# First stage in another order: the mask's copy, the choice of chunks, and the low part of the query weights

## The chip, the cores and the metric

One core of one Trainium2 chip. The core has TensorE (PE: matrix products and transposes), VectorE (DVE), ScalarE (ACT), GpSimd (POOL) and SyncE (SP), which issues the DMAs here. Each engine runs its own instructions in order and waits on semaphores for the others. The metric is the time of one execution on the device in microseconds (us).

## The reference

A Perceiver-like layer in float32. Only the first step matters here.

```
x: (16, 64, 512)   ctx: (16, 1601, 512)   mask: (1, 1, 64, 1601), int32, 0 = hidden
n = (x - mean) / sqrt(var + 1e-5)
q = n @ w_q.T ; k = ctx @ w_k.T ; v = ctx @ w_v.T          16 heads of 32
s = q . k / sqrt(32) ; s = where(mask == 0, -1e9, s)
x = x + softmax(s) @ v @ w_o.T
x = x + self-attention of norm(x) with LoRA terms
x = x + gated mixture of 20 experts (top 2) of norm(x)
```

With the given inputs the mask is 0 for the first part of the keys and 1 behind it, the same for all 64 queries.

## The kernel before

The keys are padded to 2000 and cut into 5 chunks of 400. The program looks at the mask and works out which chunks hold an unmasked key for some query; only those are computed. In the given data one chunk is left, and the branches for more chunks are jumped over.

Products in full float32 accuracy are made of three matmuls in the faster type float32r: each operand is split in a high part (a rounding copy, on ScalarE) and a low part (source minus high part, on VectorE, `rest`). `mm3` issues the three (lines 186 to 188). `weight_hi` and `weight_lo` do this for whole weights of 128x2048, `turn_x` for the transposed x, `context` for the context.

The first stage runs as follows.

- SyncE (`sync`) issues, in this order, the constants, the mask in two copies (one for partitions 0 to 63, one for 64 to 127, into the room of `qc`, named `mska`), the first half of x, wq, the second half of x, wk, and the LoRA factors. The mask's copy reads `in_mask`, laid out chunk by chunk, so that a partition's row of 2000 words comes in 5 pieces of 1600 bytes. Then SyncE waits for `v_ids` 4, loads the chunk's number from `ids` and issues the context of the first batch element (`craw`), two copies for `cap` and one for `excl`, then, behind `v_w` 1, wv into the room of wq.
- VectorE waits for the mask, reduces it to one flag per chunk (`cm`, L1092), makes a flag for rows without any key (`rows`), and writes `fl`. TensorE transposes `fl` into bank 7 (L263), VectorE reduces it to `fr`, TensorE multiplies it with a triangle of ones (L265), VectorE reads the result into `frow` (L1108), and twelve small instructions (L1111 to L1119) turn it into the list of chunks and their count, `ids`. The statistics of x tiles 0 and 1 (`bn`, L1079 and L1081) lie in the gaps of this exchange.
- Then VectorE does the statistics of tiles 2 and 3, the variance (L1085), waits for GpSimd's power -0.5 (L1631), scales (L1124), normalises tiles 0 and 1 (`apply_x`, L1088), makes wq's low part, and takes the four transposed tiles as they come (`turn_x`). After these come the context's low part, wk's low part, the same work for x tiles 4 to 7, wv's low part, `make_cap`, and the LoRA factors' blocks (L1294, L1297).
- TensorE transposes the tiles (L192), multiplies the LoRA factors (L420), does the query products of tiles 0 to 3 (`queries(0)`, 48 matmuls), transposes tiles 4 and 5, does two of four key products of the first batch element, transposes tiles 6 and 7, does the other two, and then `queries(1)`. Behind that is the loop over 16 batch elements (`cross(0)`).
- ScalarE makes wq's high part, copies the four transposed tiles, then the context's high part, wk's and wv's, and then empties the banks of the query products.
- GpSimd does nothing in this stage but the two powers (`power`); afterwards it scales the attention's weights.

`v_w` counts low parts of weights made on VectorE; wk's is the second, wv's the third, wo's the fourth. The order on each engine is written by hand.

Near the end the mixture of experts gathers tokens with GpSimd's DMAs into `xi`, a ring of X = 11 buffers, X - 1 of them ahead.

## Time and profile before

| | |
|---|---|
| median of 3 runs | 786.26 us (784.39 to 786.62) |
| profiled execution | 786.06 us |
| its span | 784.2 us |
| PE busy | 710.7 us (91%) |
| DVE busy | 412.2 us (53%) |
| ACT busy | 362.4 us (46%) |
| POOL busy | 280.5 us (36%) |
| DMA | 72.61 MB, mean 93 GB/s |

The times of the trace are counted from the span's start. PE is the engine of the matmuls; PEld are its weight loads, which run beside them; SPq is the queue of SyncE, which issues DMAs. A timeline line gives start, duration, engine, line of the code, operation, what is written and read with its shape, the number of instructions merged into the line, and in brackets how long the engine had stood idle before and what ended that. A line of busy time by stretch gives from:to, the length, the busy time (and number of instructions) of PE, PEld, DVE, ACT and POOL in this order, the granted clock of TensorE as a share of 2.4 GHz, the busy share of the 16 DMA engines, and the GB/s that they moved. The list of DMA issues gives the number of copies, the size of one and the median time from issue to landing.

### The profile page before, as it was taken

Reading aid. Unit: us, or ns where it says so; the run is one execution under the profiler, and the core shown is the slowest. Engines: PE = TensorE matmul, PEld = TensorE weight load, DVE = VectorE, ACT = ScalarE, POOL = GpSimd, SP = SyncE. Lnnn points to the kernel's source line nnn. Section 1 sums busy time; section 2 is a strip of 40 time slices with the busy share of each in tenths; the row PEclk is TensorE's granted clock in tenths of the full one; section 3 lists DMA queues with packets and bytes.
Section 4 is the critical chain, followed back from the end, with each engine's and each line's share of the span. In section 5 each row is a group of like instructions: output and inputs, shape, how many; then the busy total and the mean of one; then the engine's idle time right before and its main releaser. Section 6 shows DMA issues by size and latency. Waiting matters only on the chain.

```text
span 784.2 us, 17023 instructions
## 1 busy us (share of the span) xinstructions
PE 710.7 (91%) x6845; PEld 586.5 (75%) x6845; DVE 412.2 (53%) x950; ACT 362.4 (46%) x662; POOL 280.5 (36%) x256
## 2 busy tenths in 40 slices
PE   0899999999999999999999999999999745999970
PEld 0697888878878887889887877887778644788860
DVE  4833344453444324544454236635476557599965
ACT  1425344553545344534454244434365240499950
POOL 0005145413553245324542353613125212566530
PEclk9999999999999999999999999999999975799995
DMA  9401101211121101110110002110001753499918
GB/s 288 148 1 43 44 2 44 97 69 35 38 97 43 44 1 43 43 44 2 43 43 3 2 3 73 59 63 2 2 17 43 267 186 133 166 373 389 338 53 321
DMA packets 29585, 72.61 MB, mean 93 GB/s; under 512 B 3917, under 2 KB 4941, under 8 KB 28472
## 3 DMA queue, kind: packets, MB, share of 16 engines
q1 hardware_dynamic: 25096, 63.00, 22.9%
q0 software_dynamic: 4400, 8.41, 3.0%
q8 instruction: 58, 0.95, 0.5%
q14 instruction: 31, 0.25, 0.1%
HBM read 66.14 MB, written 11.27 MB: 99 GB/s over the span
## 4 chain that ended last, share of the span: by engine, by line
PE 85%; DVE 5%; issue 4%; ACT 2%; DMA 2%; SPq 0%; POOL 0%; DVEq 0%; POOLq 0%; ACTq 0%
PE bank L186 22%; PE bank L188 20%; PE bank L187 20%; PE bank L192 10%; PE bank L345 4%; PE bank L322 3%; DMA wr<-scratch_ys 1%; PE bank L644 1%; PE bank L560 1%; PE bank L656 1%; PE bank L547 1%; PE bank L576 1%; DVE wh L1072 1%; DVE stats L1326 0%; ACT wh L751 0%
## 5 line engine op out<-in xcount | busy, mean ns | idle before, releaser
L1641 POOL TENSOR_SCALAR pp<-pp,rl 128x400 f32<-128x400 f32 x128 | 163.8, 1297 | 234.8 <-DVE rl L1169 234.8
L1224 DVE COPY pt<-bank 128x512 f32<-128x512 f32 x64 | 44.3, 692 | 99.4 <-PE bank L192 99.3
L186 PE MATMUL bank<-chi,wk 128*128 128x400 f32 x256 | 93.5, 365 | 0.0
L834 ACT ACTIVATE pp<-pp,acc 128x400 f32<-128x400 f32 x128 | 79.0, 620 | 28.0 <-DVE acc L1257 27.7
L1257 DVE CUSTOM_DVE_ANT_0 pp<-bank,cap 128x400 f32<-128x400 f32 x128 | 66.8, 569 | 46.5 <-PE bank L322 46.5
L188 PE MATMUL bank<-chi,wk 128*128 128x400 f32 x256 | 88.3, 345 | 0.0
L187 PE MATMUL bank<-clo,wk 128*128 128x400 f32 x256 | 88.3, 345 | 0.0
L186 PE MATMUL bank<-wv,chi 128*128 128x512 f32 x200 | 83.5, 417 | 0.0
L188 PE MATMUL bank<-wv,clo 128*128 128x512 f32 x200 | 78.5, 393 | 0.0
L187 PE MATMUL bank<-wv,chi 128*128 128x512 f32 x200 | 78.5, 393 | 0.0
L751 ACT ACTIVATE pt<-bank 128x512 f32<-128x512 f32 x64 | 38.2, 597 | 76.4 <-PE bank L192 75.3
L192 PE MATMUL bank<-cst,pp 128*128 128x128 f32 x512 | 67.2, 274 | 0.6 <-DVE x_sb L1201 0.6
L186 PE MATMUL bank<-wh,xu 128*128 128x512 f32 x152 | 65.1, 428 | 1.0 <-issue 1.0
L192 PEld LDWEIGHTS bank<-cst,pp 128*128 128x128 f32 x512 | 58.5, 140 | 5.8 <-issue 0.8
L188 PE MATMUL bank<-wh,xu 128*128 128x512 f32 x152 | 61.8, 407 | 0.0
L187 PE MATMUL bank<-wh,xu 128*128 128x512 f32 x152 | 61.6, 405 | 0.0
L751 ACT ACTIVATE vv<-bank 128x512 f32<-128x512 f32 x50 | 29.1, 583 | 65.0 <-PE bank L188 65.0
L186 PEld LDWEIGHTS bank<-wv,chi 128*128 128x128 f32 x200 | 37.5, 187 | 28.0 <-issue 19.4
L1156 DVE COPY kk<-bank 128x400 f32<-128x400 f32 x32 | 18.4, 575 | 63.3 <-PE bank L188 63.3
L187 PEld LDWEIGHTS bank<-clo,wk 128*128 128x128 f32 x256 | 48.3, 189 | 0.0
L186 PEld LDWEIGHTS bank<-chi,wk 128*128 128x128 f32 x256 | 48.2, 188 | 0.0
L188 PEld LDWEIGHTS bank<-chi,wk 128*128 128x128 f32 x256 | 48.1, 188 | 0.0
(244 smaller groups left out, 1394.2 us busy)
## 6 DMA issues: line engine op xcount, KB each, us to landing
wr<-in_We SPq DMA_DIRECT2D x13, 1024.0 KB
craw<-in_ctx SPq DMA_DIRECT2D x16, 800.0 KB, 4.3
raw<-in_We SPq DMA_DIRECT2D x8, 1024.0 KB
acc<-in_We SPq DMA_DIRECT2D x6, 1024.0 KB
wr<-scratch_ys SPq DMA_DIRECT2D x8, 512.0 KB, 7.6
x_sb<-in_x SPq DMA_DIRECT2D x2, 1024.0 KB, 11.8
scratch_xn<-acc SPq DMA_DIRECT2D x8, 256.0 KB, 2.6
out_dram<-x_sb SPq DMA_DIRECT2D x8, 256.0 KB, 5.7
```

The costliest lines, as they stand in the source:

```text
L186: pe.matmul(o, lhs[0], rhs[0], start=start, stop=False)
L187: pe.matmul(o, lhs[0], rhs[1], start=False, stop=False)
L188: return pe.matmul(o, lhs[1], rhs[0], start=False, stop=stop)
L192: last = pe.transpose(bank[0:n, k * 128:(k + 1) * 128], of(k), ident)
L322: last = pe.matmul(scores[64 * c:64 * c + 64, j, :], qc[r, 2 * half + c, 64 * b:64 * b + 64], kk[r, 2 * half + c, :], start=True, stop=True)
L345: last = pe.matmul(turned[32 * j:32 * j + 32, g, :], vv[:, (25 * (n // 8) + 3 * (n % 8) + i4) % 4, 128 * g + 32 * j:128 * g + 32 * j + 32] ...
L751: return act.activation(dst, src, ACT.Copy)
L834: act.activation(frame(p8), frame(p8), ACT.Exp, bias=bias, scale=-1.0, accum_out=total).then_inc(S["a_exp"], 1)
L1156: dve.tensor_copy(kk[:, g, :], at("k", 4 * n + g)[:, 0:CW]).then_inc(S["v_k"], 1)
L1224: dve.tensor_copy(pt[:, p8 % 4, :, :].rearrange("p a c -> p (a c)"), at("t", 8 * (n - 1) + p8)[:, :]).then_inc(S["v_pt"], 1)
L1257: dve.tensor_tensor_reduce(out=frame(p8), in0=scores[:, p8 % 4, :], in1=cap[:, :], scale=-1.0, scalar=nm[:, b, p8:p8 + 1] if seg else 3e38 ...
L1641: pool.tensor_scalar(frame(p8), frame(p8), rl[:, n % 2, p8:p8 + 1], None, ALU.mult).then_inc(S["g_pn"], 1)
```

## The change

Five edits, all but the last in the first stage.

1. The mask is read from a new input `rows`, the same data laid out by query, so that a partition's row is one piece of 8000 bytes. `cap` still reads `in_mask`.
2. On VectorE all four bn pairs and the variance come directly behind `rows`; `fl` is made behind the variance, `fr` behind that, `frow` is read behind the second normalise.
3. The twelve small instructions that make `ids` are a function `used()`, called behind the fourth `turn_x`, in front of the context's low part.
4. wq's low part is made on GpSimd, behind the first power, in four instructions of 128x512, with its own semaphore `g_w`. The counts of `v_w` fall by one. SyncE's copy of wv waits for `g_w`. TensorE does `queries(0)` before the LoRA products instead of behind them.
5. X, the number of `xi` buffers, is 10 instead of 11.

```diff
--- before.py
+++ after.py
@@ -21,7 +21,7 @@
     NB, D, T, CW, PW, NC_, E, X8 = 16, 512, 1024, 400, 112, 5, 20, 15
     EPS = 1e-5
     SCALE = 32.0 ** -0.5
-    R, X, EARLY, SPLIT, BLOCKS = 8, 11, 4, 9, 35
+    R, X, EARLY, SPLIT, BLOCKS = 8, 10, 4, 9, 35
     LAST, LEAD = E + X8, 96
 
     root = ExitStack()
@@ -164,7 +164,7 @@
 
 
         names = """d_cst d_x0 d_x1 d_ctx d_cap d_xn d_raw0 d_raw1 d_par
-            v_own p_ids v_ids g_rstd v_mv v_var v_xn p_xt a_xt v_xt a_w v_w p_q a_q g_own g_zero
+            v_own p_ids v_ids g_rstd v_mv v_var v_xn p_xt a_xt v_xt a_w g_w v_w p_q a_q g_own g_zero
             a_ctx v_ctx p_k a_k v_k p_v a_v p_s v_max a_exp p_t a_pt v_pt p_pv v_o v_cap v_cor a_cor v_rl g_pn v_dg p_dg  v_lora s_bar
             a_h v_h g_h p_o v_x1 s_redo v_r g_r g_ln a_nx p_n a_n v_n2 p_wl a_wl v_wl p_bl v_bl p_qd a_qd v_qd
             p_kT a_kT p_v2 a_v2 a_w2 v_w2 g_we g_xb p_sc v_sm a_e2 v_rl2 g_p2 p_t2 a_t2 p_a2 a_h2 v_h2 p_pj v_x2 p_n2 a_n2
@@ -271,7 +271,7 @@
                 turn4(pe, pb[5 + i % 2], lambda k: xn[:, i % 2, k * 128:(k + 1) * 128]).then_inc(S["p_xt"], 1)
 
             def queries(hf):
-                pe.wait_ge(S["v_w"], 1)
+                pe.wait_ge(S["g_w"], 1)
                 pe.wait_ge(S["v_xt"], 4 * hf + 4)
                 for m in range(4):
                     for ready in freed("q", 4 * hf + m):
@@ -283,7 +283,7 @@
 
             def k_part(n, g):
                 c = columns(n)
-                pe.wait_ge(S["v_w"], 2)
+                pe.wait_ge(S["v_w"], 1)
                 pe.wait_ge(S["v_ctx"], n + 1)
                 for ready in freed("k", 4 * n + g):
                     pe.wait_ge(*ready)
@@ -293,7 +293,7 @@
                 last.then_inc(S["p_k"], 1)
 
             def v_part(n, j):
-                pe.wait_ge(S["v_w"], 3)
+                pe.wait_ge(S["v_w"], 2)
                 if j % 25 % 3 == 0 and j % 25 not in (0, 24):
                     pe.wait_ge(S["v_ctx"], n + 2)
                 for ready in freed("v", j):
@@ -414,13 +414,13 @@
 
             for i in range(4):
                 turn_x(i)
+            queries(0)
             pe.wait_ge(S["d_par"], 16)
             pe.wait_ge(S["v_ids"], 3)
             for j in range(2):
                 last = pe.matmul(pb[7][:, j * 128:(j + 1) * 128], lora[:, 2 * j, :], lora[:, 2 * j + 1, :], start=True,
                                  stop=True)
             last.then_inc(S["p_ids"], 1)
-            queries(0)
             turn_x(4)
             turn_x(5)
             k_part(0, 0)
@@ -1095,28 +1095,21 @@
             dve.wait_ge(own.sem, own.n)
             own.on(dve.tensor_reduce(rows[:, 0:1], cm[:, :], AX.X, ALU.max))
             dve.wait_ge(own.sem, own.n)
-            dve.tensor_scalar(rows[:, 1:2], rows[:, 0:1], SCALE, None, ALU.mult)
+            own.on(dve.tensor_scalar(rows[:, 1:2], rows[:, 0:1], SCALE, None, ALU.mult))
             own.on(dve.tensor_scalar(rows[:, 2:3], rows[:, 0:1], -1.0, 1.0, ALU.mult, ALU.add))
-            dve.wait_ge(own.sem, own.n)
-            dve.tensor_scalar(fl[:, 0:NC_], cm[:, :], rows[:, 2:3], None, ALU.max).then_inc(S["v_ids"], 1)
-            dve.wait_ge(d_x[0], 16)
-            own.on(bn(0))
-            dve.wait_ge(S["p_ids"], 1)
-            dve.tensor_reduce(fr[:, :], pb[7][0:NC_, 0:128], AX.X, ALU.max).then_inc(S["v_ids"], 1)
-            own.on(bn(1))
-            dve.wait_ge(S["p_ids"], 2)
-            dve.tensor_copy(frow[:, 0:10], pb[7][0:1, 0:10]).then_inc(S["v_ids"], 1)
-            dve.wait_ge(S["v_ids"], 3)
             dve.wait_ge(S["d_cst"], 16)
-            own.on(dve.tensor_tensor(frow[:, 10:15], frow[:, 0:5], cst[0:1, 142:147], ALU.mult))
-            for j in range(NC_):
+
+            def used():
+
+                own.on(dve.tensor_tensor(frow[:, 10:15], frow[:, 0:5], cst[0:1, 142:147], ALU.mult))
+                for j in range(NC_):
+                    dve.wait_ge(own.sem, own.n)
+                    own.on(dve.scalar_tensor_tensor(out=frow[:, 15:20], in0=frow[:, 5:10], scalar=float(j + 1),
+                                                    in1=frow[:, 10:15], op0=ALU.is_equal, op1=ALU.mult,
+                                                    accum_out=frow[:, 20 + j:21 + j]))
                 dve.wait_ge(own.sem, own.n)
-                own.on(dve.scalar_tensor_tensor(out=frow[:, 15:20], in0=frow[:, 5:10], scalar=float(j + 1),
-                                                in1=frow[:, 10:15], op0=ALU.is_equal, op1=ALU.mult,
-                                                accum_out=frow[:, 20 + j:21 + j]))
-            dve.wait_ge(own.sem, own.n)
-            dve.tensor_copy(ids[:, 0:5], frow[:, 20:25]).then_inc(S["v_ids"], 1)
-            dve.tensor_copy(ids[:, 5:6], frow[:, 9:10]).then_inc(S["v_ids"], 1)
+                dve.tensor_copy(ids[:, 0:5], frow[:, 20:25]).then_inc(S["v_ids"], 1)
+                dve.tensor_copy(ids[:, 5:6], frow[:, 9:10]).then_inc(S["v_ids"], 1)
 
 
             def scaled(i, n):
@@ -1267,17 +1260,24 @@
                             share(n, p8 // 2 - 1, seg)
                     share(n, 3, seg)
 
-            own.on(bn(2))
-            own.on(bn(3))
+            dve.wait_ge(d_x[0], 16)
+            for i in range(4):
+                own.on(bn(i))
             variance(0, 4)
+            dve.tensor_scalar(fl[:, 0:NC_], cm[:, :], rows[:, 2:3], None, ALU.max).then_inc(S["v_ids"], 1)
+            dve.wait_ge(S["p_ids"], 1)
+            dve.tensor_reduce(fr[:, :], pb[7][0:NC_, 0:128], AX.X, ALU.max).then_inc(S["v_ids"], 1)
             scaled(0, 4)
             apply_x(0)
             apply_x(1)
-            weight_lo(wh[0], raw[:, 0], 1)
+            dve.wait_ge(S["p_ids"], 2)
+            dve.tensor_copy(frow[:, 0:10], pb[7][0:1, 0:10]).then_inc(S["v_ids"], 1)
             for i in range(4):
                 turn_x(i)
                 if i < 2:
                     apply_x(i + 2)
+            dve.wait_ge(S["v_ids"], 3)
+            used()
             context(0)
             weight_lo(wk, raw[:, 1], 2)
             dve.wait_ge(d_x[1], 16)
@@ -1642,6 +1642,11 @@
                                            ALU.mult).then_inc(S["g_pn"], 1)
 
             power(0, 4, (S["v_var"], 1), S["g_rstd"])
+            pool.wait_ge(S["a_w"], 1)
+            pool.wait_ge(d_raw[0], 16)
+            for k in range(4):
+                ins = pool.tensor_tensor(wh[0][1][:, k, :], raw[:, 0, k, :], wh[0][0][:, k, :].bitcast(f32), ALU.subtract)
+            ins.then_inc(S["g_w"], 1)
             power(4, 4, (S["v_var"], 2), S["g_rstd"])
             pool.wait_ge(S["p_q"], 8)
             alone(pool.memset(pp[:, 0:8 * D].rearrange("p (t c) -> p t c", t=8)[:, :, 0:PW], 0.0))
@@ -1752,7 +1757,7 @@
         def sync(sp):
             sp.dma_start(cst[:, :], t["cst"]).then_inc(S["d_cst"], 16)
             for h in range(2):
-                sp.dma_start(mska[64 * h:64 * h + 64, :, :], t["mask"].rearrange("c q k -> q c k")).then_inc(S["d_cap"], 16)
+                sp.dma_start(mska[64 * h:64 * h + 64, :, :], t["rows"]).then_inc(S["d_cap"], 16)
             xv = t["x"].rearrange("(i b) q d -> i (b q) d", b=2)
             sp.dma_start(x_sb[:, 0:4, :], xv[0:4].rearrange("i p d -> p i d")).then_inc(d_x[0], 16)
             sp.dma_start(raw[:, 0], t["wq"]).then_inc(d_raw[0], 16)
@@ -1789,18 +1794,18 @@
                 for b in range(NB - 1):
                     context(16 * seg + b + 1, b + 1, chunk)
                     if seg == 0 and b == 4:
-                        sp.wait_ge(S["v_w"], 3)
+                        sp.wait_ge(S["v_w"], 2)
                         sp.dma_start(raw[:, 0], t["wo"]).then_inc(d_raw[0], 16)
                     if seg == 0 and b == 5:
                         sp.dma_start(raw[:, 1], t["w2q"]).then_inc(d_raw[1], 16)
                     if seg == 0 and b == 7:
-                        sp.wait_ge(S["v_w"], 4)
+                        sp.wait_ge(S["v_w"], 3)
                         sp.dma_start(raw[:, 0], t["w2k"]).then_inc(d_raw[0], 16)
 
             chunk = chunk_of(0)
             context(0, 0, chunk)
             load_cap(chunk, 0)
-            sp.wait_ge(S["v_w"], 1)
+            sp.wait_ge(S["g_w"], 1)
             sp.dma_start(raw[:, 0], t["wv"]).then_inc(d_raw[0], 16)
             sp.wait_ge(S["v_ids"], 5)
             count = sp.value_load(ids[0:1, 5:6], min_val=1, max_val=5)
@@ -1973,6 +1978,7 @@
         "x": v["x"],
         "ctx": ctx.reshape(16, NC, CW, 4, 128).transpose(0, 1, 4, 3, 2),
         "mask": mask.reshape(64, NC, CW).transpose(1, 0, 2),
+        "rows": mask.reshape(64, NC, CW),
         "excl": excl,
         "cst": cst,
         "cs2": cs2,
```

## Rows read from the trace of the kernel before

**Rows 1.** the page's chain of work that ended last, its share of the span by engine.

```profile
PE 85%; DVE 5%; issue 4%; ACT 2%; DMA 2%; SPq 0%; POOL 0%; DVEq 0%; POOLq 0%; ACTq 0%
```

**Rows 2.** busy time of each engine by stretch (columns as told above).

```profile
28.00:41.00 13.00, 13.00 (x49) 10.27 (x49) 11.38 (x17) 5.59 (x6) 1.02 (x1) 1.00 0.19 64
...
60.00:475.00 415.00, 413.04 (x4453) 341.69 (x4452) 175.35 (x460) 189.54 (x428) 164.82 (x130) 1.00 0.11 37
```

**Rows 3.** the same view, three stretches of the first 23 us.

```profile
2.50:10.00 7.50, 0.00 (x0) 0.00 (x0) 0.00 (x0) 0.00 (x0) 0.00 (x0) 1.00 0.98 220
...
10.00:15.00 5.00, 0.57 (x3) 0.16 (x3) 4.78 (x12) 0.04 (x1) 0.00 (x0) 1.00 1.03 403
...
21.00:23.00 2.00, 1.23 (x6) 0.83 (x4) 2.00 (x2) 1.19 (x2) 0.00 (x0) 1.00 0.87 219
```

**Rows 4.** timeline of VectorE, 10 to 18 us.

```profile
10.02 2.24 DVE L1092 TENSOR_REDUCE cm<-qc 128x5 f32<-128x2000 int32 x1 [10.02 <-DMA qc<-in_mask]
...
12.94 0.23 DVE L1101 TENSOR_SCALAR fl<-cm,rows 128x5 f32<-128x5 f32 x1
...
15.03 0.15 DVE L1111 TENSOR_TENSOR frow<-frow,cst 1x5 f32<-1x5 f32 x1
...
16.33 0.67 DVE L1079 BATCH_NORM_STATS2 stats<-x_sb 128x6 f32<-128x512 f32 x1
...
18.05 0.17 DVE L1085 TENSOR_SCALAR rstd<-mv 128x4 f32<-128x4 f32 x1
```

**Rows 5.** DMA of the context: SyncE's timeline, and the list of issues.

```profile
17.35 0.36 SPq L1770 DMA_DIRECT2D craw<-in_ctx  x1
...
craw<-in_ctx SPq DMA_DIRECT2D x16, 800.0 KB, 4.3
```

**Rows 6.** timeline, all engines, 19 to 28 us.

```profile
19.66 1.00 DVE L1088 TENSOR_SCALAR xn<-x_sb,mv,rstd 128x512 f32<-128x512 f32 x2
...
20.26 1.97 PE L192 MATMUL bank<-cst,xn 128*128 128x128 f32 x8 [5.87 <-DVE xn L1088]
...
21.41 0.60 ACT L751 ACTIVATE xt<-bank 128x512 fp32r<-128x512 f32 x1 [4.54 <-PE bank L192]
...
23.38 0.54 DVE L1088 TENSOR_SCALAR xn<-x_sb,mv,rstd 128x512 f32<-128x512 f32 x1
...
26.80 0.69 DVE L1072 TENSOR_TENSOR xt<-bank,xt 128x512 fp32r<-128x512 f32 x1 [0.36 <-ACT xt L751]
...
27.64 0.77 PE L186 MATMUL bank<-xt,wh 128*128 128x512 f32 x1 [0.36 <-DVE xt L1072]
```

**Rows 7.** timeline, all engines, 26 to 48 us.

```profile
26.67 1.53 ACT L751 ACTIVATE chi<-craw 128x1600 fp32r<-128x1600 f32 x1
...
28.23 1.83 DVE L1072 TENSOR_TENSOR clo<-craw,chi 128x1600 fp32r<-128x1600 f32 x1 [0.73 <-ACT chi L751]
...
32.24 0.69 DVE L1079 BATCH_NORM_STATS2 stats<-x_sb 128x6 f32<-128x512 f32 x1
...
37.14 1.00 DVE L1088 TENSOR_SCALAR xn<-x_sb,mv,rstd 128x512 f32<-128x512 f32 x2
...
40.94 1.03 PE L192 MATMUL bank<-cst,xn 128*128 128x128 f32 x8
...
43.92 0.54 DVE L1088 TENSOR_SCALAR xn<-x_sb,mv,rstd 128x512 f32<-128x512 f32 x1
...
47.01 0.43 PE L186 MATMUL bank<-chi,wk 128*128 128x400 f32 x1
```

**Rows 8.** groups of GpSimd's instructions: count | busy us, mean ns of one | idle before.

```profile
L1704 POOL TENSOR_TENSOR wh<-raw,wh 128x512 fp32r<-128x512 f32 x4 | 5.1, 1290 | 0.0
```

**Rows 9.** TensorE's idle time and clock near 618 us: timeline, then stretches.

```profile
618.06 0.66 PE L192 MATMUL bank<-cst,acc 128*128 128x128 f32 x4 [2.38 <-ACT acc L901]
...
615.80:619.20 3.40, 1.14 (x7) 1.06 (x8) 0.40 (x3) 1.26 (x2) 0.74 (x2) 1.00 1.00 288
...
619.20:622.60 3.40, 3.40 (x9) 2.67 (x9) 2.38 (x6) 0.15 (x1) 0.58 (x2) 0.50 1.05 386
```

## The prediction, made blind

> **What bounds the kernel now.** I read the chain of waits first: TensorE has 85% of it [rows 1]. Then the busy times by stretch: from 28 to 41 us TensorE is busy in all of 13.00 us, and from 60 to 475 us in 413.04 of 415 [rows 2]. So from the first query product at 27.64 [rows 6] to the end of the attention over the chosen chunk TensorE hardly waits, and whatever shifts it in the first stage shifts the end by as much. The change touches nothing behind that but one buffer (11 to 10 of `xi`). The question is when TensorE starts, and how long it idles afterwards. The clock column tells a second thing: after TensorE had been busy for 1.14 of 3.40 us (an idle 2.38 us among them) the granted clock fell to 0.50 for the next 3.4 us, the lower of its two levels, 1.2 GHz [rows 9]. Idle time can cost twice.
>
> **The start of VectorE.** It waits for the mask until 10.02 [rows 4]. Call the mask's landing m. The copy's two halves write 64 partitions each. In 2.5 to 10 us the 16 DMA engines moved 220 GB/s, in 10 to 15 us, x and the query weights on 128 partitions, 403 [rows 3]. Spread over 16 engines, a piece of 1600 B at 220 GB/s takes 116 ns and a piece of 2048 B of x at 403 takes 81 ns: the shorter piece is slower, so its length can't be the whole reason. The stretch of the next copies on 64 partitions (`cap`) shows 219 again [rows 3]. New copy: pieces of 8000 B, still 64 partitions. The mask is 128 x 2000 words of 4 B [rows 4], 1.02 MB. Ends for m: 10.0 (nothing gained; 10.6 if four long pieces per engine balance worse) and 7.0 (the 1.02 MB at 403 instead of 220 GB/s saves 2.1 us, and up to 0.9 more for fewer pieces). The nearest row is `cap`'s, so I stay near the upper end: m = 9.1. x comes right behind: 1.05 MB at 403 GB/s are 2.6 us, less than the 2.92 us that VectorE needs from m to the end of the `rows` work (10.02 to 12.94 [rows 4]).
>
> The Trainium skill, "SBUF — State Buffer", section "Door 1: The DMA port swizzle", says that bandwidth goes by how many of 16 ports the partitions reach, and its formula gives 64 neighbouring partitions half of them. By that rule a longer piece brings hardly anything, m is 9 to 10, and it speaks against this part of the change. The two rates of rows 3 (220 and 403) agree with it; no row separates it from the length of the pieces.
>
> **The order on VectorE.** Behind the 2.92 us come four bn pairs: the last two take 16.33 to 18.05, 0.86 each, so 3.44. From the variance to the first normalised tile there are 18.05 to 19.66, 1.61 [rows 4, 6]; GpSimd's power lies in it, and over it now lies the round of `fl`, TensorE and `fr`, which hides there (one transpose and a short reduce; up to 0.2 us if not). Sum: first tile at m + 8.0 = 17.1, before 19.66. Taken out of this path are the reads of `frow` and `ids` (15.03 to 16.33, six small operations and two casts [rows 4]).
>
> From the first tile to the third were 3.72 us, with the low part of the query weights between; without it VectorE waits for nothing but the hand-overs TensorE, ScalarE, VectorE. Normalising starts 0.6 ahead of its transposes (19.66, 20.26), ScalarE's copy follows 1.15 later (21.41) and takes 0.6, the subtraction 0.7: 3.05 us [rows 6]. From there to the end of the last subtraction 23.38 to 27.49 [rows 6], 4.1. So the four transposed tiles are ready at m + 15.1 = 24.2 and the queries start at 24.3, 3.3 us earlier than now.
>
> **GpSimd.** Four subtractions of 128x512 at 1.290 us, the same operation and types as in [rows 8], are 5.2 us. They begin behind the power at m + 7.6 and end at m + 12.8, 2.3 us ahead of the tiles: costs nothing. At 1.5 us each it still ends ahead. If this cover goes, the queries start later by the rest, and that falls into the idle time shown below, so up to 3 us late it would still cost nothing.
>
> **What is moved behind.** `used()` now follows the fourth subtraction. In the kernel before, the operation at 15.03 led to the issue of the context's copy at 17.35, 2.3 us [rows 4, 5]: 1.3 on VectorE (to 16.33, with the casts) and 1.0 in SyncE's wait and value load. New: m + 15.1 + 2.3 = m + 17.4 = 26.5, where it was 17.35. Behind this issue in SyncE's queue are the copies for `cap`, `excl` and wv, all needed later. The context lands a median of 4.3 us after its issue [rows 5]; I take 4.4, m + 21.8. Before, it had landed long before ScalarE was free for it, so its whole transfer was hidden; now it is exposed. Queued behind it on ScalarE are the high parts of wk and wv; on VectorE, in this order, the context's low part, wk's low part, the second half's bn, its variance, and only then the fifth normalised tile, for which TensorE waits.
>
> ScalarE's copy of the context takes 1.53 us, and VectorE's part starts at m + 23.4. From there the order stands as it is: 28.23 to 32.24 the low parts of the context and wk, to 37.14 the bn, power and scaling [rows 7]: 8.91 us. The fifth tile starts at m + 32.3 = 41.4 (now 37.14) and its transposes 0.6 later at 42.0. Now they start at 40.94 [rows 7], when TensorE gets to them: there the tile is 3.2 us early, and this slack is used up and 1.1 more.
>
> TensorE has 13.3 us of query products (27.64 to 40.94) and then four LoRA products of 128 columns, about 0.5 (eight transposes of 128 columns took 1.03 [rows 7]). It ends at about 38.1 and idles 3.9 us, whatever m is. After the idle 2.38 us of [rows 9] it ran 3.4 us at half clock, which is 1.7 us of work lost. I add 1.7, with bounds of 0 (the low stretch lies in the idle time) and 3.
>
> **Sum.** From the transposes to the end of the next pair, 40.94 to 47.01, are 6.1 us [rows 7]. New: 42.0 + 6.1 + 1.7 = 49.8, which is 2.8 us later. VectorE sets a floor under this: the eighth tile at 43.92 shifts by 4.3 to 48.2, and its transposes end 1.0 later at 49.2. So without the clock's loss it would be +2.2, a wait in place of 1.1 of it. Behind this point TensorE has no holes and 2.8 us go through. The `xi` buffer costs nothing: its gathers run nine blocks ahead instead of ten, and a shorter memset hides beside TensorE; I put at most 0.3 us either way. The profiled execution took 786.06 (span 784.2 and 1.9 around it), 0.2 below the median of 786.26; so 788.9 for it, 789.1 for the median.
>
> **Rivals.**
> - *Forecast* (chance 0.50): 789.1, own range 787.6 to 790.8.
> - *The mask's copy runs at the full rate* (0.32), not slower. m is 7.4 or less; everything behind it moves 1.7 earlier, the transposes start at 40.3, and the sum is +1.1 (with no clock loss VectorE's floor leaves +0.5): 786.8 to 787.4. For it: the copy had 640 pieces and now has 128. Against it: the 116 and 81 ns. It decides from m below about 8.7, where the loss falls under 2.4 us.
> - *The context's landing does not bind* (0.06), faster. TensorE keeps its 3.3 us earlier start: 783.0. It needs the fifth tile's transposes at 37.6, 4.4 us earlier than my sum, which only an m of 4.7 would give, below every bound that I have. For it: until now this part of the work was hidden with 3.2 us to spare.
> - *No gain on the mask, and the low clock lasts two stretches* (0.12): m = 10.0 gives +3.7, and 1.7 more: 790.0 to 791.6.
>
> **Numbers.** 0.3% is 2.4 us, about what a measurement can tell from no change. Faster by more: the third case and the spread of the runs, 0.07. Within: the second case and the lower fifth of the first, 0.41. Slower: 0.52. The range leaves out most of the third case and the end of the last: 785.8 to 791.3.
>
> **What would show it.** The mask's reduce starts at about 9.1 (between 8.6 and 10 for the half-partition reading, at 7.4 for the length); the first query product at 24 to 25; the context's issue 17.4 us behind the reduce's start; VectorE idle for some 6 us in front of the context's low part; one hole of 3 to 4.5 us in TensorE between the LoRA products and the fifth tile's transposes, its releaser the normalised tile, and a granted clock of 0.50 behind it. From the third group of key products on (47.01 before) every line shifts by one constant, 2 to 4 us. The forecast is wrong if the hole is absent, or if the queries' low part on GpSimd is what releases the first query product.

## The result and the profile after

| | before | after |
|---|---|---|
| median of 6 runs each | 786.71 us (784.39 to 788.22) | 792.14 us (789.89 to 795.39) |
| ratio of the two | | 1.0074 (95% interval 1.0055 to 1.0093) |
| profiled execution, its span | 786.06, 784.2 us | 795.39, 793.6 us |
| first product with attention weights (L345) starts | 82.4 us | 89.8 us |

The change costs 5.4 to 5.8 us; 2.8 were forecast (789.1), and the time lies outside the range. The profiled execution of after is the slowest of its six, so its span overstates the loss; where it matters, the execution of `undo_rows` below stands beside it, which does the same work.

The page's chain of waits for after: TensorE's share falls from 85% [rows 1] to 83%, VectorE's rises from 5% to 7%, and the DMA's is 2% in both.

```profile
PE 83%; DVE 7%; issue 4%; DMA 2%; ACT 2%; POOL 0%; SPq 0%; DVEq 0%; POOLq 0%; ACTq 0%
```

Busy time by stretch for after, columns as in [rows 2]. The loop's long stretch is as full as before (413.48 of 415 us), so what is lost by then lies ahead of it: 7.4 us at L345. The other 2.0 us of this execution come behind that stretch (below, at one_copy, on the clock). The mask's stretch moves 220 GB/s, to the digit what it moved before [rows 3].

```profile
2.50:10.00 7.50, 0.00 (x0) 0.00 (x0) 0.00 (x0) 0.00 (x0) 0.00 (x0) 1.00 0.98 220
...
60.00:475.00 415.00, 413.48 (x4397) 342.46 (x4397) 173.79 (x457) 190.13 (x429) 164.83 (x130) 1.00 0.11 37
```

The start, as a timeline of after (all engines). The mask's reduce starts at 10.10, not at 9.1: no gain shows. The variance follows at 16.22, where m + 6.4 would be 16.5, so that part of the working held. Then comes what was not expected: the scaling of 128x4 takes 1.24 us (0.23 before), and two normalises 2.86 instead of 1.00 [rows 6], while GpSimd's four subtractions run beside them from 17.52. The subtraction from PSUM at 22.12, which also runs beside GpSimd, keeps its 0.69. The queries start at 27.35: 17.25 us behind the mask, not 15.2.

```profile
10.10 2.24 DVE L1092 TENSOR_REDUCE cm<-qc 128x5 f32<-128x2000 int32 x1 [10.10 <-DMA qc<-in_rows]
...
16.22 0.17 DVE L1085 TENSOR_SCALAR rstd<-mv 128x4 f32<-128x4 f32 x1
...
17.52 5.30 POOL L1648 TENSOR_TENSOR wh<-raw,wh 128x512 fp32r<-128x512 f32 x4
...
17.57 1.24 DVE L1117 TENSOR_SCALAR rstd<-rstd,rows 128x4 f32<-128x4 f32 x1 [0.21 <-POOL rstd L1631]
...
18.84 2.86 DVE L1088 TENSOR_SCALAR xn<-x_sb,mv,rstd 128x512 f32<-128x512 f32 x2
...
20.34 1.11 PE L192 MATMUL bank<-cst,xn 128*128 128x128 f32 x4 [2.73 <-DVE xn L1088]
...
22.12 0.69 DVE L1072 TENSOR_TENSOR xt<-bank,xt 128x512 fp32r<-128x512 f32 x1 [0.35 <-ACT xt L751]
...
27.35 0.76 PE L186 MATMUL bank<-xt,wh 128*128 128x512 f32 x1 [1.50 <-DVE xt L1072]
```

The middle of the first stage, same view. The context is issued at 29.43, 12 us later than in [rows 5]. ScalarE has it at 34.52, VectorE's part starts at 36.10, then wk, the statistics and the fifth normalise at 45.00 (37.14 in [rows 7]); TensorE has finished the LoRA products at 41.09 and stands idle for 4.51 us.

```profile
28.27 0.16 DVE L1111 CAST ids<-frow 1x5 int32<-1x5 f32 x1
...
29.43 0.36 SPq L1775 DMA_DIRECT2D craw<-in_ctx  x1
...
34.52 1.54 ACT L751 ACTIVATE chi<-craw 128x1600 fp32r<-128x1600 f32 x1 [8.04 <-DMA craw<-in_ctx]
...
36.10 1.83 DVE L1072 TENSOR_TENSOR clo<-craw,chi 128x1600 fp32r<-128x1600 f32 x1 [7.62 <-ACT chi L751]
...
37.90 2.29 DVE L1072 TENSOR_TENSOR wk<-raw,wk 128x2048 fp32r<-128x2048 f32 x1
...
40.38 0.71 PE L421 MATMUL bank<-vv 16*128 16x128 f32 x4
...
45.00 1.01 DVE L1088 TENSOR_SCALAR xn<-x_sb,mv,rstd 128x512 f32<-128x512 f32 x2
...
45.60 1.97 PE L192 MATMUL bank<-cst,xn 128*128 128x128 f32 x8 [4.51 <-DVE xn L1088]
...
54.42 0.43 PE L186 MATMUL bank<-chi,wk 128*128 128x400 f32 x1
```

The list of waits of after, 28 to 46 us, tells the same chain from the other end: engine and what it did, who released it, the sum, how often, the longest. Read upwards it is TensorE for VectorE, VectorE for ScalarE, ScalarE for the DMA. Before, the first was absent, the second 0.73 us [rows 7], and the third absent in this stretch.

```profile
ACT chi L751 <- DMA craw<-in_ctx: 8.0, 1, 8.0
...
DVE clo L1072 <- ACT chi L751: 7.6, 1, 7.6
...
PE bank L192 <- DVE xn L1088: 4.5, 1, 4.5
```

Clock: in the hole and behind it. The granted clock falls at the end of the hole (0.90 on average over it) and is 0.66 on average over the next 8.8 us: some 6 of them at 0.50, which is 1.2 GHz. The work of [rows 7] from 40.94 to 47.01, 6.07 us, takes 8.82 (45.60 to 54.42).

```profile
41.10:45.60 4.50, 0.00 (x0) 0.00 (x0) 3.19 (x10) 3.17 (x5) 1.02 (x1) 0.90 0.10 43
...
45.60:54.40 8.80, 8.79 (x40) 8.72 (x41) 7.03 (x13) 1.84 (x4) 0.00 (x0) 0.66 0.01 3
```

### The profile page after: what moved, and what is told of

It is laid out like the page before. It is cut to its first block, busy times and chain, and to the rows that moved or that the text cites. A ratio compares the mean times of both kernels' runs of the same rounds, so it can differ in the third digit from the quotient of the medians.

```text
span 793.6 us, 17027 instructions
## 1 busy us (share of the span) xinstructions
PE 714.7 (90%) x6845; PEld 589.7 (74%) x6845; DVE 412.8 (52%) x949; ACT 362.4 (46%) x662; POOL 284.2 (36%) x260
## 4 chain that ended last, share of the span: by engine, by line
PE 83%; DVE 7%; issue 4%; DMA 2%; ACT 2%; POOL 0%; SPq 0%; DVEq 0%; POOLq 0%; ACTq 0%
PE bank L186 21%; PE bank L188 20%; PE bank L187 20%; PE bank L192 10%; PE bank L345 4%; PE bank L322 3%; DMA wr<-scratch_ys 1%; PE bank L644 1%; PE bank L560 1%; PE bank L656 1%; PE bank L547 1%; DMA craw<-in_ctx 1%; PE bank L576 1%; DVE xn L1088 0%; DVE stats L1326 0%
```

## The experiments

Eleven kernels, for two questions: which part of the loss comes from where, and which mechanism is behind it. A ratio is against the kernel before on the same chip, with its 95% interval; "L345" is the start of the first product with attention weights in the profiled execution (82.4 before), which shows the first stage's shift free of what the clock does later. It still holds two things that no edit made. One is the mask's landing, 9.26 to 10.17 us over all executions with two copies. The other is a slow start of the query products: at first they follow each other every 0.43 us, later every 0.23, and the slow part lasts from 2.7 us (best) to 6.1 us (before_x10). The column of the granted clock says 1.00 all the same (27.64 to 32.05 us in before, 27.35 to 30.90 in after). before_x10 changes nothing in this stage and has 83.0 instead of 82.4, so a difference of half a microsecond in this column says nothing.

| kernel | median us | ratio | L345 |
|---|---|---|---|
| after | 792.14 | 1.0074 (1.0055 to 1.0093) | 89.8 |
| undo_rows | 790.42 (one run) | | 88.1 |
| one_copy | 790.52 | 1.0051 (1.0034 to 1.0067) | 84.5 |
| undo_pool | 791.39 | 1.0073 (1.0050 to 1.0096) | 87.2 |
| pool_sixteen | 793.18 (one run) | | 87.6 |
| half2_first | 787.52 | 1.0026 (1.0010 to 1.0042) | 83.0 |
| early_used | 788.40 | 1.0026 (1.0007 to 1.0045) | 84.1 |
| filled_hole | 790.88 | 1.0063 (1.0043 to 1.0084) | 87.4 |
| before_pool | 788.04 | 1.0021 (1.0008 to 1.0034) | 83.8 |
| before_x10 | 786.12 | 0.9998 (0.9984 to 1.0011) | 83.0 |
| before_one_copy | 782.94 | 0.9961 (0.9945 to 0.9976) | 79.1 |
| best | 781.42 | 0.9933 (0.9915 to 0.9951) | 76.6 |

The medians of the kernel before were 785.93, 786.43 and 785.95 on the three chips.

### The mask: undo_rows, one_copy, before_one_copy

undo_rows:

```diff
-                sp.dma_start(mska[64 * h:64 * h + 64, :, :], t["rows"]).then_inc(S["d_cap"], 16)
+                sp.dma_start(mska[64 * h:64 * h + 64, :, :], t["mask"].rearrange("c q k -> q c k")).then_inc(S["d_cap"], 16)
```

> The changed kernel with the mask read from the old layout again (pieces of 1600 B, two copies of 64 partitions). Theory (64 partitions bound the copy, whatever the piece): the mask's reduce starts at 10.0 to 10.2, as with the new layout (10.10), and the stretch from 2.5 to 10 us moves about 220 GB/s. Rival (the long pieces did help and something else held the mask back): it starts later than 11.

Measured: the reduce starts at 9.48, somewhat earlier than with the long pieces, and not later than 11, as the rival had it. Over the profiled executions with two copies of 64 partitions the short pieces gave 10.02, 9.94, 9.48 and 9.26, the long ones 10.10, 10.17, 9.76, 9.59, 9.52 and 9.41: no difference. The new layout brought nothing that can be seen.

one_copy, on the changed kernel (the waits on `d_cap` fall by 16 each):

```diff
-            for h in range(2):
-                sp.dma_start(mska[64 * h:64 * h + 64, :, :], t["rows"]).then_inc(S["d_cap"], 16)
+            sp.dma_start(mska[:, :, :], t["rows"]).then_inc(S["d_cap"], 16)
...
-        "rows": mask.reshape(64, NC, CW),
+        "rows": _np.tile(mask.reshape(64, NC, CW), (2, 1, 1)),
```

> The changed kernel with the mask in one copy over all 128 partitions, same pieces of 8000 B. Theory (partitions reached): the mask runs at about 400 GB/s and its reduce starts at 7.3 to 7.9; everything of the first stage moves 2.3 to 2.8 us earlier and the median falls by the same, to about 2.6 us over the kernel before. Rival (the first copies after the start are slow, or both halves read the same memory): the reduce starts at 9.5 to 10.1 and the time does not change.

before_one_copy is the same edit on the kernel before, in the old layout: the source is the chunk-by-chunk mask with its 64 rows doubled to 128, so it keeps 640 pieces of 1600 B.

> The kernel before with one edit: the mask in one copy over 128 partitions, still 640 pieces of 1600 B. Theory (partitions reached, not the pieces): the reduce starts at 6.0 to 6.6, like the 6.05 of the one copy of long pieces, the queries start at about 24, all of the first stage moves 3.4 to 4 us earlier, and the median falls by 2.5 to 4 us, to 782 to 783.5. Rival (short pieces cost by themselves): the reduce starts at 7.5 or later.

Timeline and stretch of one_copy, then of before_one_copy. Same bytes, same pieces as their parents, and the mask is there at 6.05 and 6.59; the stretch moves 397 and 378 GB/s instead of 220. So the length of the pieces was not the bound, and going from two copies of 64 partitions to one of 128 removes it. That the number of partitions is what counts is argued, not shown alone: the edit also makes one copy of two, and its source holds each row twice, where the two halves used to read the same rows. No run separates the three. Whether the pieces matter once this bound is gone is not shown either: 6.05 against 6.59 (and 6.72 in best) is less than the 0.9 us by which the mask's landing varies with two copies.

```profile
6.05 2.24 DVE L1092 TENSOR_REDUCE cm<-qc 128x5 f32<-128x2000 int32 x1 [6.05 <-DMA qc<-in_rows]
...
2.50:10.00 7.50, 0.00 (x0) 0.00 (x0) 3.81 (x8) 0.00 (x0) 0.00 (x0) 1.00 1.02 397
```

```profile
6.59 2.24 DVE L1092 TENSOR_REDUCE cm<-qc 128x5 f32<-128x2000 int32 x1 [6.59 <-DMA qc<-in_pairs]
...
2.50:10.00 7.50, 0.12 (x1) 0.09 (x1) 3.27 (x7) 0.00 (x0) 0.00 (x0) 1.00 1.04 378
```

It gained more than I expected of it (3.4 to 4.1 us at the reduce, against 2.3 to 2.8). On the kernel before the stage moves 3.3 us and the median 3.5. On the changed kernel the stage moves 3.6 us against undo_rows, but the median falls only by some 1.8 us (ratio 1.0051 against 1.0074, intervals that overlap). The granted clock shows where the rest stays. From L345 to the end of the span one_copy's profiled execution takes 703.8 us, like after (703.8), against 701.8 in before and 700.5 in undo_rows, with no edit in that stretch. In one_copy the mean clock from 610 to 690 us is 0.68, where undo_rows, after and before have 0.72. In after it is 0.83 from 485 to 505 us, where undo_rows and one_copy have 1.00 and before has 0.91.

Stretches of one_copy and undo_rows, then of after and undo_rows:

```profile
610.00:690.00 80.00, 55.99 (x300) 45.41 (x299) 47.18 (x142) 24.50 (x31) 23.00 (x25) 0.68 0.53 186
...
610.00:690.00 80.00, 55.96 (x314) 45.58 (x314) 48.12 (x146) 24.63 (x33) 22.91 (x25) 0.72 0.53 187
```

```profile
485.00:505.00 20.00, 19.30 (x95) 16.35 (x94) 15.39 (x42) 11.79 (x19) 8.13 (x16) 0.83 0.22 69
...
485.00:505.00 20.00, 19.30 (x103) 15.97 (x104) 16.14 (x46) 13.39 (x20) 9.75 (x19) 1.00 0.18 62
```

It is not only the profiled one: over the whole span all five executions of one_copy have a mean clock of 0.949 to 0.952, on average 0.9504; the six of after have 0.950 to 0.957, on average 0.954. Over 790 us that difference is some 2.8 us at the full clock (an estimate from these means), enough for what is missing. Why the clock falls for longer there is open.

### GpSimd: undo_pool, pool_sixteen, before_pool

undo_pool, on the changed kernel:

```diff
 GpSimd
-            for k in range(4):
-                ins = pool.tensor_tensor(wh[0][1][:, k, :], raw[:, 0, k, :], wh[0][0][:, k, :].bitcast(f32), ALU.subtract)
-            ins.then_inc(S["g_w"], 1)
 VectorE, behind apply_x(1)
+            dve.wait_ge(S["a_w"], 1)
+            rest(wh[0][1][:, :, :], raw[:, 0], wh[0][0][:, :, :]).then_inc(S["g_w"], 1)
```

> The changed kernel with the low part of the query weights back on VectorE, behind the second normalise. Theory (GpSimd's subtractions keep VectorE's tensor_scalar out): the scaling takes 0.23 instead of 1.24 us and the first two normalises 1.00 together instead of 2.86; the subtraction of 2.29 us comes in their place, so the queries start 0.5 to 1 us earlier than 27.35 and the fifth tile's transposes as much earlier than 45.6: 0.5 to 1 us gained. Rival (the normalises are slow for another reason, the DMA traffic or the start): they stay at 1.4 us each and the kernel gets 2 us slower.

The timeline of undo_pool: the scaling is back at 0.23, the pair of normalises at 1.00. The queries start 15.77 us behind the mask instead of 17.25, the fifth tile's transposes 33.93 instead of 35.50: 1.5 us, more than expected, since most of the 2.29 us of subtraction lies in time in which VectorE would wait for the transposed tiles anyway: it ends at 21.10, and ScalarE's copy of the first tile had ended at 20.25. The medians (1.0073 and 1.0074) can't tell it; undo_pool's five executions spread from 788.26 to 793.45.

```profile
17.63 0.23 DVE L1117 TENSOR_SCALAR rstd<-rstd,rows 128x4 f32<-128x4 f32 x1 [0.21 <-POOL rstd L1633]
...
17.90 1.00 DVE L1088 TENSOR_SCALAR xn<-x_sb,mv,rstd 128x512 f32<-128x512 f32 x2
...
18.81 2.29 DVE L1072 TENSOR_TENSOR wh<-raw,wh 128x2048 fp32r<-128x2048 f32 x1
```

pool_sixteen:

```diff
-            for k in range(4):
-                ins = pool.tensor_tensor(wh[0][1][:, k, :], raw[:, 0, k, :], wh[0][0][:, k, :].bitcast(f32), ALU.subtract)
+            for k in range(16):
+                part = slice(128 * (k % 4), 128 * (k % 4) + 128)
+                ins = pool.tensor_tensor(wh[0][1][:, k // 4, part], raw[:, 0, k // 4, part],
+                                         wh[0][0][:, k // 4, part].bitcast(f32), ALU.subtract)
```

> The changed kernel with GpSimd's subtraction in 16 instructions of 128x128 instead of 4 of 128x512. Theory (GpSimd's instruction keeps VectorE's tensor_scalar out for its whole length, so the wait is the rest of one GpSimd instruction): the scaling takes at most 0.6 us instead of 1.24 and each of the first two normalises 0.9 or less instead of 1.4, while bn and the subtractions from PSUM keep their times. Rival (the two share the bandwidth and both slow down): the two normalises still take 2.6 us or more together. GpSimd's own sum grows from 5.3 to 6 or 7 us and may end behind the tiles.

GpSimd does the same bytes in the same order in shorter instructions, for longer (7.41 us), and VectorE's loss shrinks from 1.01 to 0.20 us on the scaling and from 1.86 to 0.23 us on the two normalises. Two engines that shared a bandwidth would not do that. So VectorE waits for the rest of the GpSimd instruction that is running. The Trainium skill, "SBUF — State Buffer", section "SBUF: two separate sides", describes this as an exclusive lock on a pair of ports that VectorE and GpSimd share. This run agrees with it for a `tensor_scalar` from SBUF to SBUF; the subtraction that reads PSUM was not held back (0.69 in both). The third normalise, which runs beside GpSimd here and only at its very end in after, takes 0.81 instead of 0.54; the fourth keeps 0.53. The queries start 15.54 us behind the mask (24.95 against 9.41), no later than in undo_pool: cut small, the move to GpSimd no longer costs. The single time, 793.18, can't show it; this execution has a hole of 4.50 us and the longer low clock behind it.

```profile
16.83 7.41 POOL L1649 TENSOR_TENSOR wh<-raw,wh 128x128 fp32r<-128x128 f32 x16
...
16.87 0.43 DVE L1117 TENSOR_SCALAR rstd<-rstd,rows 128x4 f32<-128x4 f32 x1 [0.20 <-POOL rstd L1631]
...
17.34 1.23 DVE L1088 TENSOR_SCALAR xn<-x_sb,mv,rstd 128x512 f32<-128x512 f32 x2
```

before_pool is the kernel before with edit 4 of the change for the low part (four instructions on GpSimd behind the first power, `g_w`, the counts of `v_w` down by one) and with edit 5, and nothing else.

> The kernel before with the query weights' low part on GpSimd as in the change (four instructions of 128x512 behind the first power) and 10 token buffers, and nothing else changed. Theory (GpSimd's subtractions keep VectorE's tensor_scalar out): the scaling takes 1.24 instead of 0.23 us, the first two normalises 2.8 instead of 1.0, the queries start at 28.8 to 29.3 instead of 27.6, TensorE passes the shift on: 1.2 to 1.7 us slower, ratio 1.0015 to 1.0022. Rival (taking 2.3 us off VectorE pays even so): 0 to 0.7 us faster.

The prolonged instructions are there in the same sizes, and the ratio is 1.0021 (1.0008 to 1.0034), 1.7 us slower. The queries start 19.15 us behind the mask (28.41 against 9.26), 1.5 us more than before (17.62). Taken alone this part of the change is a loss, though it takes 2.3 us of work off VectorE.

```profile
18.59 5.29 POOL L1647 TENSOR_TENSOR wh<-raw,wh 128x512 fp32r<-128x512 f32 x4
...
18.64 1.24 DVE L1124 TENSOR_SCALAR rstd<-rstd,rows 128x4 f32<-128x4 f32 x1 [1.17 <-POOL rstd L1630]
...
19.91 2.85 DVE L1088 TENSOR_SCALAR xn<-x_sb,mv,rstd 128x512 f32<-128x512 f32 x2
```

### The hole: half2_first, early_used, filled_hole

half2_first:

```diff
             used()
-            context(0)
-            weight_lo(wk, raw[:, 1], 2)
             dve.wait_ge(d_x[1], 16)
             for i in range(4, 8):
                 own.on(bn(i))
             variance(4, 4)
             scaled(4, 4)
             apply_x(4)
             apply_x(5)
+            context(0)
+            weight_lo(wk, raw[:, 1], 2)
```

> The changed kernel with the statistics, scaling and the fifth and sixth normalise in front of the context's and wk's low parts on VectorE. Theory (the hole of 4.5 us and the low clock behind it come from the context's late landing, passed on through VectorE's order): no hole in front of the fifth tile's transposes, which start at about 41.1; a smaller wait of 1 to 2 us appears at the seventh tile, behind wv's low part; the clock stays at its upper level; 3 to 4 us of the 5.6 come back. Rival (the loss lies elsewhere, in the start or behind the first stage): less than 1 us comes back.

TensorE's timeline of half2_first: the fifth tile is transposed right behind the LoRA products, at 40.62, and no wait is shown; the later wait is 0.40 us, less than expected. The granted clock stays up in the whole stage. 3.8 us of the loss come back (1.0026 against 1.0074). Of the 2.0 us that stay, the first stage explains some 0.6 (L345 at 83.0); the others lie behind it, and no run here looks for them. The context still lands as late as before; only nobody stands behind it.

```profile
40.62 1.10 PE L192 MATMUL bank<-cst,xn 128*128 128x128 f32 x8
...
46.16 0.66 PE L192 MATMUL bank<-cst,xn 128*128 128x128 f32 x4
...
47.21 0.66 PE L192 MATMUL bank<-cst,xn 128*128 128x128 f32 x4 [0.40 <-DVE xn L1088]
```

early_used:

```diff
             dve.tensor_copy(frow[:, 0:10], pb[7][0:1, 0:10]).then_inc(S["v_ids"], 1)
+            dve.wait_ge(S["v_ids"], 3)
+            used()
             for i in range(4):
                 turn_x(i)
                 if i < 2:
                     apply_x(i + 2)
-            dve.wait_ge(S["v_ids"], 3)
-            used()
             context(0)
```

> The changed kernel with the choice of chunks (used) directly behind the read of frow, in front of the four transposed tiles. Theory (the loss is the context's issue, 12 us later than before, passed on through VectorE's order): the context is issued at about 24.2 instead of 29.4, the queries start about 1 us later (28.3) because VectorE does used() while TensorE waits for it, the hole behind the LoRA products shrinks from 4.1 to 4.5 us to below 1 and the low clock behind it goes; the first-stage shift against the kernel before falls from 5.7 (with one low stretch) to 1 to 2.5 us, and the median with it to 787 to 788.5. Rival (the order of used() is not what counts, the wait is for wk or for the second half of x): the hole stays above 3 us.

The context is issued at 24.49, the queries start at 28.32, and the fifth tile is ready before TensorE has done with the LoRA products: no hole. The price is that later start of the queries, 18.73 us behind the mask instead of 17.25: beside GpSimd the first operation of `used()`, a `tensor_tensor` of 1x5 with both inputs in SBUF, takes 1.03 us instead of 0.14. The time is 1.0026 (1.0007 to 1.0045), the upper end of what was expected.

```profile
24.49 0.36 SPq L1775 DMA_DIRECT2D craw<-in_ctx  x1
...
41.98 0.71 PE L421 MATMUL bank<-vv 16*128 16x128 f32 x4
...
42.61 1.09 PE L192 MATMUL bank<-cst,xn 128*128 128x128 f32 x8
```

filled_hole:

```diff
             last.then_inc(S["p_ids"], 1)
+            for k in range(16):
+                pe.matmul(pb[4][:, :], wh[0][0][:, k % 4, 0:128], xt[0][:, k % 4, :], start=True, stop=True)
             turn_x(4)
```

> The changed kernel with 16 products of 128x512 into a bank that is free, between the LoRA products and the fifth tile's transposes: about 3.8 us of work in the hole whose result nobody reads. Theory (the hole costs twice, by the wait and by the granted clock behind it): the clock stays at its upper level, the transposes still start at about 45, the third group of key products starts 1.5 to 2.9 us earlier than without the filling, and the median falls by 1 to 2.5 us. Rival (the low clock would have come anyway or costs nothing, since VectorE is late too): less than 0.6 us.

With the hole filled (4.00 us of products) the granted clock is 1.00 in the hole and behind it. From the fifth tile's transposes to the third group of key products it then takes 6.94 us, against 7.7 in undo_rows (one stretch of 3.4 us at the low clock) and 8.8 in after (two). It is not 6.07, because TensorE now waits for the seventh and eighth tile, which come late from VectorE. So the low clock costs 0.8 us net where it lasts one stretch, 1.9 where it lasts two. The median, 1.0063 against 1.0074, moves in this direction but not by more than its interval: the 1 to 2.5 us that I expected of the median are not shown.

```profile
41.28 4.00 PE L425 MATMUL bank<-xt,wh 128*128 128x512 f32 x16
...
45.10:52.10 7.00, 6.59 (x42) 5.99 (x41) 6.93 (x14) 2.19 (x4) 0.00 (x0) 1.00 0.01 4
```

Stretch of undo_rows behind its hole, for comparison:

```profile
45.00:52.80 7.80, 7.76 (x41) 7.71 (x41) 7.07 (x13) 1.89 (x4) 0.00 (x0) 0.78 0.01 3
```

### The buffer: before_x10

```diff
-    R, X, EARLY, SPLIT, BLOCKS = 8, 11, 4, 9, 35
+    R, X, EARLY, SPLIT, BLOCKS = 8, 10, 4, 9, 35
```

> The kernel before with 10 instead of 11 buffers for the gathered tokens. Theory (off the path): nothing, ratio 0.999 to 1.001. Rival (part of the loss is here): 0.5 us or more slower, with the experts' stage longer than in the kernel before.

0.9998 (0.9984 to 1.0011): nothing.

### A faster kernel: best

On the kernel before: the mask in one copy; `used()`, which is what the changed kernel calls the lines behind the read of `frow`, between the variance and the scaling; the low part of wq on VectorE in four pieces.

```diff
             variance(0, 4)
+            used()
             scaled(0, 4)
             apply_x(0)
             apply_x(1)
-            weight_lo(wh[0], raw[:, 0], 1)
+            dve.wait_ge(S["a_w"], 1)
+            for k in range(3):
+                rest(wh[0][1][:, k, :], raw[:, 0, k, :], wh[0][0][:, k, :])
             for i in range(4):
                 turn_x(i)
                 if i < 2:
                     apply_x(i + 2)
+                if i == 1:
+                    rest(wh[0][1][:, 3, :], raw[:, 0, 3, :], wh[0][0][:, 3, :]).then_inc(S["v_w"], 1)
```

> The kernel before with the mask in one copy over 128 partitions, the choice of chunks inside the wait for GpSimd's power (behind the variance, ahead of the scaling), and the query weights' low part on VectorE in pieces of 128x512, three behind the second normalise and one behind the fourth. From the rows of before_one_copy: used() costs 1.35 us that now lie in a wait of 1.34, and the pieces take 0.7 us less of the way to the third normalise; the queries start at 22.0 to 22.6 instead of 24.2, the fifth tile's transposes and all behind it 1.5 to 2 us earlier than in before_one_copy, and no hole opens. Median 780.5 to 781.5, ratio 0.992 to 0.995. Rival (the context's copy, issued 1.9 us later than in before_one_copy, ends the first stage instead): a hole of 1 us or more in front of the fifth tile, and no gain over before_one_copy (783).

781.42 us, ratio 0.9933 (0.9915 to 0.9951): 5.3 us faster than the kernel before, and by the two ratios 11 us faster than the changed one. `used()` ends at 14.84, beside GpSimd's power (13.60 to 14.65), and the queries start 15.9 us behind the mask (17.6 before). Some 0.8 us of the 5.8 at L345 are the query products' slow start, which is short in this execution (2.7 us, 4.4 before). The first stage has no hole, although the context is issued at 15.79, 1.9 us later than in before_one_copy.

```profile
6.72 2.24 DVE L1092 TENSOR_REDUCE cm<-qc 128x5 f32<-128x2000 int32 x1 [6.72 <-DMA qc<-in_pairs]
...
13.35 0.17 DVE L1085 TENSOR_SCALAR rstd<-mv 128x4 f32<-128x4 f32 x1
...
14.71 0.13 DVE L1272 CAST ids<-frow 1x1 int32<-1x1 f32 x1
...
15.02 1.00 DVE L1088 TENSOR_SCALAR xn<-x_sb,mv,rstd 128x512 f32<-128x512 f32 x2
...
15.79 0.37 SPq L1774 DMA_DIRECT2D craw<-in_ctx  x1
...
22.61 0.76 PE L186 MATMUL bank<-xt,wh 128*128 128x512 f32 x1 [0.35 <-DVE xt L1072]
...
28.00:41.00 13.00, 13.00 (x70) 11.50 (x69) 10.22 (x23) 3.28 (x6) 1.02 (x1) 1.00 0.05 17
```

## Why the prediction was wrong

The direction was right, and so was the path: the context's late issue comes through ScalarE and VectorE to a hole in TensorE. The step that failed is "GpSimd ... costs nothing": it cost 2 us on that path. Three terms were too small besides: the mask's landing, the context's landing and the clock. The loss is twice the forecast. Step by step:

- **m = 9.1**: failed. Measured 10.1 (9.4 to 10.2 over the executions listed above). Of my two readings the likelier one, bound by partitions and not by pieces, was the right one, yet I still granted 0.9 us for fewer pieces. No gain shows in any execution. This is 0.3 to 1.1 us of the miss. The Trainium skill, "SBUF — State Buffer", section "Door 1: The DMA port swizzle", gives 64 neighbouring partitions half of the ports; 220 GB/s with two such copies and 397 with one of 128 partitions agree with it.
- **Four bn pairs and `fl` in the power's shadow, m + 6.4 to the variance**: right (16.22 - 10.10 = 6.1).
- **GpSimd "costs nothing"**: this is the step that failed. I asked only whether GpSimd would end in time, and it did (22.82, the queries start at 27.35). I took VectorE's durations beside it from rows where GpSimd was idle. The scaling and the two normalises grew by 2.9 us, and the queries came 2.05 later than forecast (17.25 instead of 15.2 us behind the mask). All that the low part taken off VectorE was to bring there was 0.7 us (3.72 to 3.05 in my sum).
- **The cover of the first tiles**: I wrote that a later start of the queries would fall into the idle time. True for the queries, false for `used()`, which hangs on the same four tiles: 1.9 of the 2.05 us went through `used()`, the context's issue, and all of VectorE's order to the fifth tile.
- **`used()` to the issue, 2.3 us; issue to landing, 4.4**: 2.3 measured (27.12 to 29.43), 5.1 for the landing (29.43 to 34.52). 0.7 of the miss. I took the median of the sixteen copies (4.3); `cap`, `excl` and wv are issued within 2.4 us behind this one, and whether they slow it is not tested.
- **8.91 us from the context's low part to the fifth normalise**: 8.90 (36.10 to 45.00). **Idle 3.9 us**: 4.51, and 4.11 in undo_rows. It came this near because both ends of the hole moved, by 3.0 and 3.6 us.
- **1.7 us for the clock**: measured 2.75 in after, 1.7 in undo_rows. Five traces have the hole. Behind 3.60, 3.77 and 4.11 us without work (one_copy, undo_pool, undo_rows) the granted clock stays at 0.50 for 3.4 to 3.5 us; around the end of 4.50 and 4.51 us (pool_sixteen, after) for 6.8, from 0.7 to 0.9 us before the hole ends. So a hole longer by 0.4 us may be what cost the second stretch, but no run was made for it, and five traces don't settle it. The spread of the six runs, 5.5 us, is far more than this 1.05 us: the fastest has a mean clock of 0.957, the slowest, which is the profiled one, 0.950, and part of that lies at 485 to 505 us.
- **`xi`, nothing**: right, before_x10.

Added up for the third group of key products, in the profiled execution: 2.8 forecast, + 1.0 for the mask, + 1.92 for what GpSimd did (measured where `used()` starts: 17.02 us behind the mask instead of 15.1), + 0.69 for the landing, - 0.03 for the two steps behind it, + 1.05 for the clock give 7.43; the rows show 7.41 (47.01 to 54.42). For undo_rows, with its mask at 9.48 and one low stretch, the third group starts at 52.77, 5.8 us later than before, close to what the median moved. All misses have the same sign; none hid another.

Of the rivals, the one with no gain on the mask and two low stretches (790.0 to 791.6) came nearest, and was still short by the GpSimd term, which no rival held. Two things stay open: why the granted clock is low for longer behind the first stage in one_copy, which kept half of its earlier start from the median, and which of the three differences between two copies and one makes the mask land sooner.

## What to carry to other kernels

When work moves from VectorE to GpSimd, don't ask only whether GpSimd ends in time. List what VectorE runs beside it: an SBUF to SBUF `tensor_scalar` of 0.5 us was held up by about 1 us beside GpSimd instructions of 1.3 us, and short GpSimd instructions make that wait short. Before a step is moved behind another to clear a path, follow what it issues: here a DMA whose 4 to 5 us had been hidden came out in front of an in-order queue, and putting independent work ahead of the wait (half2_first) brought back two thirds. A copy that fills 64 neighbouring partitions twice should be one copy over 128.

## What the runs showed of the hardware

- From 2.5 to 10 us, two copies of 64 neighbouring partitions each, one behind the other, go at 220 GB/s, with pieces of 1600 or of 8000 B; with one copy of 128 partitions the stretch has 378 (1600 B) and 397 GB/s (8000 B).
- GpSimd's subtraction of 128x512 takes 1.25 to 1.45 us and is hardly slowed by the VectorE instructions that it holds up (5.30 us for four, against 5.16 for the same four in [rows 8]); cut in 16, it takes 7.41 us.
- After 3.6 to 4.1 us without work TensorE's granted clock was 0.50 (1.2 GHz) for 3.4 to 3.5 us in three executions; with 4.5 us without work it was so for 6.8 us in two.
- The first query products follow each other every 0.43 us and later every 0.23, a ratio of 1.8 like that behind the hole at the two levels of the clock (0.33 and 0.18 us for 400 columns), yet the column of the granted clock says 1.00. The spacing of equal products shows more there than the column does.
